# Top-2 experts of a graph network on one Trainium2 core: from every expert for every node to 32 pages of 256 routed rows per layer, weights addressed by register

## The reference, cut to what matters

```python
h = x @ W_in + b_in
for l in range(L):
    agg = segment_sum(h[src], dst, N) / deg
    logits = concatenate([h, agg], -1) @ router_W[l] + router_b[l]     # 8 experts
    vals, idx = top_k(logits, 2)
    gates = softmax(vals)
    gate_dense = zeros_like(logits).at[rows, idx].set(gates)
    weak = relu(einsum('nh,ehf->nef', agg, weak_W[l]) + weak_b[l])     # 4 experts, 256 -> 256
    sh = relu(einsum('nh,ehf->nef', agg, strong_W1[l]) + strong_b1[l]) # 4 experts, 256 -> 512
    strong = einsum('nef,efh->neh', sh, strong_W2[l]) + strong_b2[l]   # 512 -> 256
    moe = einsum('ne,neh->nh', gate_dense, concatenate([weak, strong], 1))
    h = h + sigmoid(h @ conf_W[l] + conf_b[l]) * moe
return x + h @ W_out + b_out
```

## Time and profile before

| | us |
|---|---|
| median of the runs | 3162.29 |
| the profiled execution: its own time is known as its span | 3158.2 |
| TensorE busy with matmuls | 2940.0 (93%) |
| VectorE busy | 2182.3 (69%) |
| ScalarE busy | 942.8 (30%) |
| GpSimd busy | 16.7 (1%) |
| the experts' three layers, from the barrier to the output stage | about 1612 to 3126 |

### The profile page before, as it was taken

How to read it: one execution, slowest core, us unless ns; L and a number is a source line. 1 busy time by engine, 2 the same in 40 slices (tenths; PEclk the granted TensorE clock), 3 DMA queues, 4 the chain that set the end, 5 groups by cost and what they waited for, 6 DMA issues and landing times. The chain is left out here.

```text
span 3158.2 us, 47679 instructions
## 1 busy us (share of the span) xinstructions
PE 2940.0 (93%) x18758; PEld 1775.7 (56%) x18758; DVE 2182.3 (69%) x4012; ACT 942.8 (30%) x1776; POOL 16.7 (1%) x23
## 2 busy tenths in 40 slices
PE   2888889999998999999989999989999999999997
PEld 1566555556454544544556666655666665666665
DVE  7999565557346777776667666777767677766676
ACT  3888522113211000000032222343323234323223
POOL 2000000000000000000000000000000000000000
PEclk8899999999999999999989999999999999999999
DMA  5445367776006554554330000020000002000001
GB/s 130 141 142 160 107 188 211 218 232 198 23 1 204 154 171 153 166 156 129 93 117 4 4 4 4 3 84 4 4 7 4 3 21 67 4 4 4 4 3 43
DMA packets 310959, 265.85 MB, mean 84 GB/s; under 512 B 32767, under 2 KB 289409, under 8 KB 308174
## 3 DMA queue, kind: packets, MB, share of 16 engines
q1 hardware_dynamic: 296558, 259.28, 27.0%
q10 hardware_dynamic: 13760, 2.61, 0.4%
q0 software_dynamic: 416, 0.85, 0.1%
HBM read 172.67 MB, written 90.05 MB: 83 GB/s over the span
## 5 line engine op out<-in xcount | busy, mean ns | idle before, releaser
L1948 PE MATMUL psum<-r_wd,room_a 128*128 128x512 fp8e4 (+1 forms) x2600 | 569.5, 375 | 1.0 <-ACT r_ht L286 1.0
L2526 PE MATMUL psum<-counts,m_h 128*128 128x512 fp8e4 (+2 forms) x2100 | 417.9, 355 | 13.5 <-DVE m_h L2241 8.0
L2590 PE MATMUL psum<-m_weights,x_nodes 128*128 128x256 f16 (+1 forms) x3600 | 415.4, 273 | 12.5 <-DVE m_wtmp L2349 10.2
L2571 PE MATMUL psum<-room_a,m_weights 128*128 128x512 f16 (+2 forms) x2016 | 411.5, 356 | 14.6 <-ACT x_nodes L2481 8.6
L1948 PEld LDWEIGHTS psum<-r_wd,room_a 128*128 128x128 f16 x2600 | 241.7, 97 | 295.9 <-ACT r_ht L286 1.1
L2590 PEld LDWEIGHTS psum<-m_weights,x_nodes 128*128 128x128 f16 (+1 forms) x3600 | 352.1, 99 | 65.1 <-DVE m_wtmp L2349 9.6
L2473 ACT ACTIVATE m_agg<-psum,x_nodes 128x512 f32<-128x512 f32 (+2 forms) x336 | 239.4, 718 | 292.9 <-PE psum L2571 290.1
L2526 PEld LDWEIGHTS psum<-counts,m_h 128*128 128x128 f16 x2100 | 206.0, 99 | 208.9 <-issue 11.5
L2571 PEld LDWEIGHTS psum<-room_a,m_weights 128*128 128x128 f16 x2016 | 193.7, 99 | 214.5 <-issue 40.2
L2493 ACT ACTIVATE m_hT<-m_hT,room_a 128x256 f32<-128x256 f32 x300 | 135.7, 500 | 553.4 <-DVE m_hT L2363 553.4
L2349 DVE SCALAR_TENSOR_TENSOR m_wtmp<-psum,x_nodes,room_a 128x256 f32<-128x256 f32 (+1 forms) x300 | 144.8, 483 | 137.9 <-PE psum L2590 136.5
(11 more groups left out here) (311 smaller groups left out, 3381.2 us busy)
## 6 DMA issues: line engine op xcount, KB each, us to landing
r_wd<-packed_sym SPq DMA_DIRECT2D x120, 640.0 KB, 4.1
packed_counts<-strip SPq DMA_DIRECT2D x21, 1800.0 KB, 7.8
sym_blocks<-packed_counts SPq DMA_DIRECT2D x88, 384.0 KB, 4.8
packed_sym<-sym_blocks SPq DMA_DIRECT2D x84, 384.0 KB, 3.6
w_stage<-in_L_gnn_strong_W SPq DMA_DIRECT2D x12, 1024.0 KB, 6.6
m_weights<-in_L_gnn_strong_W SPq DMA_DIRECT2D x21, 512.0 KB, 4.7
x_parked<-x_nodes SPq DMA_DIRECT2D x2, 1600.0 KB, 5.9
x_nodes<-x_parked SPq DMA_DIRECT2D x2, 1600.0 KB, 6.3
```

Source lines behind the costliest of these rows:

```text
L1948: m = pe.matmul(bank[pair[b]][:, 0:2 * cw], h16[:, part, p0 + i, :], f_[:, 2 * b:2 * b + 2, :], start=(p0 + i == 0 and part == 0), stop=(p ...
L2526: m = pe.matmul(bank[kb][:, 0:cw], h16[:, part, i, kb * P:(kb + 1) * P], A[:, i, c_:c_ + cw], start=(i == 0 and part == 0), stop=(i == NT ...
L2571: m = pe.matmul(bank[4 + hh % 2][:, 0:cw], w_[:, i, kb, f * P:(f + 1) * P], agg16[:, j, kb, 0:cw], start=(x_ == 0), stop=(x_ == len(todo) ...
L2590: m = pe.matmul(bank[b_][0:r_, 0:H], s_[:, pa[0] * BANK + k * P:pa[0] * BANK + k * P + r_], w_[:, pa[1], f, :], start=(f == 0 and pa == PA ...
```

## The change

`block_experts` is written anew. A layer has three parts now.

1. **Routing ahead of the edge sums.** The router's half for `agg` is linear, so `h` is first multiplied with it (`inputs`, L2764, with the half for `h` and the confidence in the same 17 columns), and the eight numbers per node (as two float16 parts) are summed over the edges: `input_sums` (L2772), 25 matmuls of 16 columns per source tile. VectorE then chooses for all nodes at once (`choose`), TensorE counts ranks within each expert (`ranks`), and VectorE gives each node two slots (`assign`): each expert gets whole pages of 256 slots, 32 pages in all, whichever are full.
2. **Edge sums by destination tile** (`edges`, L2785): a piece of `A` as weights, 256 moving columns of `h16`, 50 matmuls per tile. ScalarE and VectorE write the high and low part of `agg` side by side as rows of 512 float16, and GpSimd scatters the 128 rows of a tile twice (an indirect DMA for each choice, L2377) to `slot_rows` in HBM. The last tile has 53 rows and is padded to 64 in this scatter. In the same time `slot_ones` and `sum_slots` build the list that says to which node and choice a slot belongs, and the weights are split.
3. **Pages.** SyncE loads a page (256 rows). TensorE turns it (8 transposes), then does 24 matmuls for 512 hidden columns and 24 for the output, all of 256 columns. The page's expert is read from memory into a register; the addresses of its weights and biases come from that register. A weak expert uses the same two steps: two weak experts share a piece, and the second matrix is a scaled identity that picks one. VectorE writes the result, GpSimd scatters it by node and choice to `y_rows` in HBM (L2383), two indirect DMAs a page. At the start of the next layer (and of the output) SyncE loads both rows of each node and VectorE adds them with the two gates.

The output bias is added to `x` on GpSimd at the start of the block, before `x` is parked; in the output stage, which goes tile by tile now, VectorE's addition of it is gone. Small inputs are loaded in other pieces, among them `1/deg` by node. Semaphores of earlier blocks are given back and cleared. The core of the diff:

```diff
-                ORDER = [("w1", 0), ("w1", 1), ("w2", 0), ("w2", 1), ("w1", 2), ("ww", 0), ("ww", 1), ("w2", 2), ("w1", 3), ("w2", 3)]
+    PG = 2 * P
+    SUB = PG // P
+    PAGES = (2 * N + NE * (PG - 1)) // PG
...
+            def pool_layer(l):
+                if l == 0:
+                    pool.wait_ge(rows_blank, 16)
+                pool.wait_ge(e_slots, l + 1)
+                for i in range(NT):
+                    r_ = P if i < NT - 1 else SENT
+                    pool.wait_ge(e_rows_low, l * NT + i + 1)
+                    for k in range(2):
+                        pool.indirect_dma_start(out=slot_rows, out_offset=bass.IndirectOffsetOnAxis(ap=at_list[0:r_, k, i:i + 1], axis=0),
+                                                in_=rows16[i % AR][0:r_, :], in_offset=None).then_inc(agg_out[i % AR], 16)
+                pool.wait_ge(l_listed, l + 1)
+                for j in range(PAGES):
+                    for s in range(SUB):
+                        pool.wait_ge(p_y, (l * PAGES + j) * SUB + s + 1)
+                        pool.indirect_dma_start(out=y_rows[l], out_offset=bass.IndirectOffsetOnAxis(ap=y_row[:, j * SUB + s:j * SUB + s + 1], axis=0),
+                                                in_=ysb[j % 2][s], in_offset=None).then_inc(y_out[j % 2], 16)
...
+                def hidden(j, bi):
+                    for h in range(2):
...
+                        vec.scalar_tensor_tensor(whole[:, fs, :], ps, k_hidden, b1s[:, bass.ds(col + 2 * h, 2)][:, :, None].to_broadcast([P, 2, PG]),
+                                                 ALU.mult, ALU.add).then_inc(p_wide, 1)
+                    for h in range(2):
...
+                        vec.scalar_tensor_tensor(hid[j % 2][1][:, part], tmp[j % 2][:, part], 0.0, hid[j % 2][0][:, part], ALU.max,
+                                                 ALU.subtract).then_inc(p_low, 1)
...
+                def input_sums(i):
+                    pe.wait_ge(u_low, l * NT + i + 1)
+                    of = u16[:, i].rearrange("p e x -> p (e x)")
+                    for d in (0, NT - 1, *range(1, NT - 1)):
+                        r_ = rows_of(d)
+                        m = pe.matmul(SUMS[0:r_, d * 2 * NE:(d + 1) * 2 * NE], A[:, i, d * P:d * P + r_], of, start=(i == 0 and d == 0),
+                                      stop=(i == NT - 1 and d == NT - 2))
...
+                def edges(k):
+                    for i in range(NT):
...
+                        for x_ in range(2):
+                            m = pe.matmul(bank[k % EB][0:r_, 0:H], A[:, i, k * P:k * P + r_], h16(i)[:, x_ * H:(x_ + 1) * H],
+                                          start=(i == 0 and x_ == 0), stop=(i == NT - 1 and x_ == 1))
...
+                def page_of(j):
+
+                    v = pe.value_load(codes[0:1, j:j + 1], min_val=0, max_val=8 * MOST + NBI - 1)
+                    return pe.snap((v & 7) * (2 * SL)), pe.snap((v >> 3) * H)
+
+                def hidden(j, first):
...
+                    for f in range(FB):
+                        o_ = bank[j % 2 * 2 + f // 2][:, f % 2 * PG:(f % 2 + 1) * PG]
+                        for kb in range(KB):
+                            for part in range(2):
+                                w_ = w16[:, bass.ds(first + (SPECIAL * H + part * SL + kb * BANK + f * P), P)]
+                                for y_ in range(2 - part):
+                                    m = pe.matmul(o_, w_, x[:, y_, kb, :], start=(kb == 0 and part == 0 and y_ == 0),
+                                                  stop=(kb == KB - 1 and part == 1))
...
+                def outputs(j, second):
+                    for s in range(SUB):
...
+                        for f in range(FB):
...
+                            for part in range(2):
+                                w_ = w16[:, bass.ds(second + part * SL + f * H, H)]
+                                for y_ in range(2 - part):
+                                    m = pe.matmul(out_bank(t)[:, 0:H], hid[j % 2][y_][:, at:at + P], w_, start=(f == 0 and part == 0 and y_ == 0),
+                                                  stop=(f == FB - 1 and part == 1))
...
+                for j in range(PAGES):
+                    if j + 2 < PAGES:
+                        turn_page(j + 2)
+                    if j + 1 < PAGES:
+                        hidden(j + 1, next_at[0])
+                    outputs(j, at[1])
+                    at = next_at
+                    if j + 2 < PAGES:
+                        next_at = page_of(j + 2)
```

1249 lines of the change are left out of this document (706 added, 543 removed).

## The result

| | us |
|---|---|
| before, median of the runs beside the change | 3162.23 (3160.22 to 3167.54) |
| after, median | 2888.24 (2882.01 to 2892.33) |
| ratio after / before | 0.9133, 95% interval 0.9115 to 0.9151 |
| span of the profiled execution after | 2890.0 |

What follows compares the result with a forecast made beforehand. TensorE was taken as the bound, its sequencer setting the page pace. Per layer 55 + 148 + 9 + 2 + 240 = 454; three are 1362, output 42 makes 1404; 1612 + 1404 + 4.1 = 3020 us, range 2840 to 3200.

Steps and rivals of the forecast that it cites:

- What bounds the kernel, what is removed: Whole kernel: TensorE bounds it, busy 2940.0 of 3158.2 us; the experts' 1033.5 us of matmuls are removed.
- Experts, TensorE's array: Pages: 48 matmuls at 112.5 ns and 8 transposes at 60 ns take the array 5.9 us a page.
- Experts, TensorE's sequencer: Pages: 24 fused register instructions at 181 ns, loads, waits and 56 matmuls take 7.5 us a page, setting the pace.
- Other engines in a page: Pages: VectorE up to 6.0 us, ScalarE 3.1, GpSimd 2.5 a page; none decides at 7.5.
- Edge sums: Each layer: 1250 matmuls at 112.5 ns plus ranks and slot lists, 148 us; choose, assign and scatters hidden.
- Start of a layer: Before edge sums: VectorE decides at 1.8 us a tile over TensorE's 1.6; with lead and last sums 55 us.
- Handover: Edge sums to pages: evictions, scatters landing, page load and turn take 9 us, plus 2 to fill the page pipeline.
- Output: Output stage: 8.2 us lead, VectorE's 1.25 us per tile and 3 us last store give 42 us in place of 32.
- The bias and the small loads ahead: Bias on GpSimd lies beside the first tiles; small loads before the experts cost nothing under some 600 us of relation work.
- A: Rival: register instructions cost less, array or VectorE decides; pages 5.9 to 6.1 us, total 2886 down to 2866; chance 0.28.
- C: Rival: pages cost 7.5 us, but choose and assign are late or starts take 2.5 us a tile; 3100 us; chance 0.13.
- B: Rival: register-addressed matmuls are slow in themselves, 51 ns more each; 9.95 us a page, total 3255; chance 0.17.

Runs made afterwards that it cites:

- fixed_address: The change, but TensorE takes every page's weights from one fixed address, with no page-number load or register instruction on TensorE; 2888.15 us, ratio 0.9131.
- more_registers: The change with 16 more fused register instructions a page on TensorE, addresses of a page's first half worked out by eight further operations; 3106.76 us, ratio 0.983.
- y_loads_ahead: The change, but all y_rows loads of a start or the output issued at once, later groups into the weights' room, weights loaded afterwards; 2858.48 us, ratio 0.9035.
- late_bias: The change, but the output bias is added on VectorE in the output stage and x is parked at once; 2886.28 us, ratio 0.9127.
- tail_53_rows: The change, but the last tile's two scatters take its 53 rows instead of the padded 64; 2902.90 us, ratio 0.9178.

## Why the prediction was right, and where it was not

- **What bounds the kernel, what is removed:** right. TensorE's work falls, TensorE stays the bound.
- **Experts, TensorE's array** (5.9 us a page): nearly right, 5.7. A matmul took 109 ns in place of 112.5, and the 8 transposes 0.45 us.
- **Experts, TensorE's sequencer** (7.5 us a page): this is the step that failed. The term 24 x 0.181 was mis-sized: the price came from one row of one instruction on another engine's queue, a first use that also stood behind a load, and the fused instruction in the loop takes 46 ns, some 85 with what surrounds it. The load took 0.30 for 0.49. With these the sequencer needs some 5.0 us by the estimate above, and the array decides, as fixed_address shows (nothing gained without register work) and more_registers confirms from the other side (8.0 us a page with twice as many in `hidden`, and longer ones). The term is 171 us too high, more than the 126 by which the sum was.
- **Other engines in a page:** right that none decides; VectorE is busy for 137.74 of 183.50 us.
- **Edge sums** (148 us): 142.5. `choose` and `assign` were hidden as predicted, and TensorE never waited at the seventh tile (143.00 us busy of 143.00).
- **Start of a layer** (55 us): too low by 4.5 to 13 us. Two terms failed. TensorE's share of a tile was priced from rows at the full clock, 1.6 us (1.43 as measured there), but it is at 0.50 here and takes 2.06; the prediction considered the clock for the handover alone. And in layers 2 and 3 the lead was 10.5 us for 8.2, with two more waits for loads behind it, 1.6 us at the fourth tile and 2.9 near the end; both are gone in y_loads_ahead, whose turns take 47.2 us. From the last turn to the first edge sum it was 5.3 us for 2.
- **Handover** (9 + 2 us): 12.7, its chain as listed; only because the last tile is padded, 17.5 otherwise.
- **Output** (42 us): 68.9, 27 us too low, next to 30 for the three starts together. The 1.25 us of VectorE a tile was taken as the pace, but two buffers made it wait 31.6 us for loads. That it was this is shown by y_loads_ahead, 48.9.
- **The bias and the small loads ahead:** at nothing, as said; the bias costs 2.6 us in layer 1, by slowing VectorE down, and saves 2. It was said to lie beside the first tiles; nobody waits for it, but it is not free.
- **Rivals.** A names the right mechanism: the register instructions cost less, and the array decides. But its 2886 is not the array's number: it belongs to VectorE's pace, 6.1 us a page, while the array's 5.9 gave 2866. The agreement of 2886 to 2 us is luck, a sum of errors: pages 37 us less than 96 x 6.1, edge sums 17 and the step to the median 6 less, and starts, handover and output 62 us more. Of C the half is true: a tile of a start takes longer than 1.8 us, by the clock and not by handshakes. B is refuted by fixed_address. Faster by over 0.2% had 0.8, and that came true; the forecast's own 3020 was 132 us too high, and the range held the time because it was drawn down to A.

## What to carry to other kernels

Price an instruction that repeats in a loop from a row in which it repeats; a single first use gave 181 ns here for an instruction that takes 46 in the loop, some 85 with what surrounds it, and that was more than the whole miss. A stage of many small matmuls can run at half the clock from its first tile to its last, as every start of the change did: price its tile at both levels (2.06 and 1.43 us here) before calling another engine its bound, and put no extra work in it. When a stage is rewritten to be fed by loads, count its buffers against the landing time; giving the loads dead space elsewhere was worth 1% here, more than anything done on the engines.

## What the runs showed of the hardware that was not expected

- Fused register instructions between matmuls cost TensorE nothing while its sequencer stays under the array (46 ns each, 24 a page, 2888.15 us without them and 2888.24 with them), and they became the bound with 16 more a page and all 32 of `hidden` longer, 112 ns each (8.0 us a page).
- The granted clock fell from 1.00 to 0.50 with no idle before it, in a row of float32 transposes and matmuls of 16 and 17 columns, and two matmuls of 512 columns in each 1.83 us kept it at 1.00 for the start.
- Three small operations of VectorE took 0.72, 0.84 and 1.53 us in place of 0.16 and 0.17 where GpSimd added float32 tensors at the same time; others between them kept their 0.15 us (late_bias).
- A scatter of 53 rows took 4.6 us longer to land than one of 64 (6.89 against 2.29 us, tail_53_rows).
